# An attention and mixture-of-experts layer: the small transfers of the score maxima issued by ScalarE instead of SyncE

## What is computed

```
h   = layernorm(x)
q,k,v = h @ Wq, h @ Wk, h @ Wv        # 16 heads of size 64
p   = softmax(causal(q @ k.T / 8))    # 512 x 512 per head
y   = layernorm(h + concat(p @ v) @ Wo) * gamma + beta
x   = x + y
h2  = layernorm(x)
w   = top 8 of 32 experts of softmax(h2 @ gate.T), renormalised
x   = x + sum over experts of w_e * (up_e(h2) * silu(gate_e(h2))) @ down_e.T
```

## Time and profile before

| | kernel before |
|---|---|
| median of 3 runs | 1696.54 us |
| the profiled execution, device time | 1698.83 us |
| its span | 1697.0 us |
| PE busy | 1611.1 us (95%) |
| DVE busy | 1428.4 us (84%) |
| POOL busy | 1413.8 us (83%) |
| ACT busy | 1399.0 us (82%) |
| granted TensorE clock | 0.99 of full speed |
| DMA queues in use | one, 53.6% of the 16 engines' span |

### The profile page before, as it was taken

The page is one execution under the profiler, slowest core; times in us unless marked ns, Lnnn a source line. Parts: engine busy times, 40 slices in busy tenths (PEclk is TensorE's granted clock), DMA queues, the critical chain, the costliest instruction groups (busy, mean ns, idle before and its releaser), DMA issues.

```text
span 1697.0 us, 56373 instructions
## 1 busy us (share of the span) xinstructions
PE 1611.1 (95%) x21209; PEld 1104.6 (65%) x21209; DVE 1428.4 (84%) x4461; ACT 1399.0 (82%) x2371; POOL 1413.8 (83%) x1183
## 2 busy tenths in 40 slices
PE   4899999999999999999999999999999999999968
PEld 1476666667666666676667666666666666666645
DVE  7889789798888988888898888989888898888745
ACT  3999888888988888798888988888888888988852
POOL 0687897979889797997979889797998979889884
PEclk8899999999999999999999999999999999999989
DMA  9754544746556384544646555374654646355423
GB/s 252 162 115 109 145 115 127 170 116 157 123 135 140 103 183 102 155 111 129 161 115 163 124 133 136 107 185 115 155 111 131 146 120 163 86 145 139 112 85 108
DMA packets 213902, 228.55 MB, mean 135 GB/s; under 512 B 20480, under 2 KB 178432, under 8 KB 213376
## 3 DMA queue, kind: packets, MB, share of 16 engines
q1 hardware_dynamic: 213632, 224.94, 53.6%
HBM read 84.89 MB, written 5.24 MB: 53 GB/s over the span
## 4 chain that ended last, share of the span: by engine, by line
PE 35%; POOL 30%; issue 10%; SPq 8%; DMA 8%; ACT 7%; DVE 3%; POOLq 0%; ACTq 0%; DVEq 0%
POOL p_lo L1484 10%; PE bank_r L393 8%; POOL expert_room L1499 8%; POOL halves L1508 8%; PE bank_s L393 8%; PE bank_x L393 5%; PE bank_u L393 4%; PE bank_v L393 4%; PE bank_g L393 4%; DMA expert_room<-comb_rows 3%; DMA score_ops<-rowmaxT 3%; SPq L317 2%; SPq L316 2%; SPq L315 2%; ACT p L850 2%
## 5 line engine op out<-in xcount | busy, mean ns | idle before, releaser
L1484 POOL TENSOR_TENSOR p_lo<-p,p_hi 128x1280 f16<-128x1280 f32 x256 | 671.3, 2623 | 111.8 <-ACT p_hi L783 110.9
L850 ACT ACTIVATE p<-bank_s,back 128x512 f32<-128x512 f32 (+1 forms) x768 | 457.7, 613 | 88.1 <-PE bank_s L393 51.4
L393 PE MATMUL bank_s<-score_ops 128*128 128x62 f16 (+10 forms) x4096 | 398.7, 233 | 19.8 <-DMA score_ops<-rowmaxT 15.7
L393 PEld LDWEIGHTS bank_s<-score_ops 128*128 128x128 f16 x4096 | 275.2, 97 | 176.6 <-ACT p L850 34.1
L783 ACT ACTIVATE p_hi<-p 128x1280 f16<-128x1280 f32 x256 | 324.2, 1266 | 3.4 <-PE bank_r L393 1.2
L1499 POOL TENSOR_TENSOR expert_room<-expert_room 128x512 f32<-128x512 f32 x240 | 304.8, 1275 | 18.0 <-DMA expert_room<-comb_rows 12.4
L1508 POOL TENSOR_TENSOR halves<-expert_room,halves 128x512 f16<-128x512 f32 x240 | 277.4, 1160 | 2.4 <-ACT halves L783 1.6
L1125 DVE CUSTOM_DVE_ANT_0 max_junk<-bank_r,mask 128x512 f16<-128x512 f32 (+3 forms) x401 | 183.3, 490 | 20.6 <-PE bank_g L393 17.9
L393 PE MATMUL bank_x<-w_hi,halves 128*128 128x128 f16 x1920 | 195.8, 219 | 3.4 <-POOL halves L1508 3.3
L783 ACT ACTIVATE halves<-expert_room 128x512 f16<-128x512 f32 x240 | 150.3, 627 | 29.7 <-POOL expert_room L1499 15.2
L393 PE MATMUL bank_x<-w_lo,halves 128*128 128x128 f16 x960 | 171.7, 219 | 0.0
(11 more groups left out here) (287 smaller groups left out, 5018.0 us busy)
## 6 DMA issues: line engine op xcount, KB each, us to landing
score_ops<-nat SPq DMA_DIRECT2D x256, 256.0 KB, 3.9
score_ops<-nat SPq DMA_DIRECT2D x512, 128.0 KB, 3.9
expert_room<-comb_rows SPq DMA_DIRECT2D x240, 256.0 KB, 3.5
xt<-in_x SPq DMA_DIRECT2D x16, 256.0 KB, 4.7
xb<-in_x SPq DMA_DIRECT2D x16, 256.0 KB, 4.0
out_y<-expert_room SPq DMA_DIRECT2D x16, 256.0 KB, 3.6
score_ops<-comb_rows SPq DMA_DIRECT2D x16, 256.0 KB, 5.1
expert_room<-in_gate_up SPq DMA_DIRECT2D x1, 2048.0 KB, 10.6
```

The lines of the kernel that those rows point to most:

```text
L393: return pe.matmul(dst, lhsT, rhs, start=start, stop=stop, skip_group_check=shared)
L850: act.activation(p32[:, h % P_SLOTS, at:at + cols], bank[score_bank(h, u)][:, 0:cols], ACT.Exp, scale=back[:, SC_SCORE:SC_SCORE + 1]).then ...
L1484: pool.tensor_tensor(p_lo[:, slot, :], p32[:, slot, :], p_hi[:, slot, :], ALU.subtract).then_inc(p_lo_done, 1)
```

## The change

`place_max` leaves SP's program and enters ACT's, with the same waits and the same two transfers. Every call of `copy_maxima(m, g, b)` in ACT's list (64 of them) is now directly followed by `place_max(m, g)`, and the 64 calls are taken out of SP's list. Nothing else is moved.

```diff
         @block.sync
-            def place_max(m, g):
-                wait(sp, score_mm, UNITS * 2 * (m * PAIRS + 2 * g + 1 - SLOTS + 1))
-                if m == 0:
-                    for slot in range(2 * g, min(2 * g + 2, SLOTS)):
-                        sp.wait_ge(rows_filled[slot], 32)
-                sp.wait_ge(rowmaxT_ready, m * QUADS + g + 1)
-                for k in range(2):
-                    home = QB[E:E + MAX_ROWS, slot_of(m, 2 * g + k)].rearrange("a b (c p) -> a (b c) p", c=C)
-                    sp.dma_start(home, rowmaxT[16 * k:16 * k + 16, :]).then_inc(max_placed[g], 16)
...
             for n in range(2, B - 2):
-                load_x(n + 2); place_max(n, 1); spread_weights(n - 2, 15); place_qk(n, 5); place_max(n, 2)
+                load_x(n + 2); spread_weights(n - 2, 15); place_qk(n, 5)
...
-                place_max(n, 3); spread_weights(n - 1, 5); spread_weights(n - 1, 6); spread_weights(n - 1, 7)
+                spread_weights(n - 1, 5); spread_weights(n - 1, 6); spread_weights(n - 1, 7)
...
-                place_max(n + 1, 0); spread_weights(n - 1, 9); spread_weights(n - 1, 10); spread_weights(n - 1, 11)
+                spread_weights(n - 1, 9); spread_weights(n - 1, 10); spread_weights(n - 1, 11)
...
         @block.scalar
+            def place_max(m, g):
+                wait(act, score_mm, UNITS * 2 * (m * PAIRS + 2 * g + 1 - SLOTS + 1))
+                if m == 0:
+                    for slot in range(2 * g, min(2 * g + 2, SLOTS)):
+                        act.wait_ge(rows_filled[slot], 32)
+                act.wait_ge(rowmaxT_ready, m * QUADS + g + 1)
+                for k in range(2):
+                    home = QB[E:E + MAX_ROWS, slot_of(m, 2 * g + k)].rearrange("a b (c p) -> a (b c) p", c=C)
+                    act.dma_start(home, rowmaxT[16 * k:16 * k + 16, :]).then_inc(max_placed[g], 16)
...
-                exps(n, 2, 1); exps(n, 2, 2); copy_maxima(n, 1, U); p_high(n, 2); gate_tanh(n - 2, 13, R1)
+                exps(n, 2, 1); exps(n, 2, 2); copy_maxima(n, 1, U); place_max(n, 1); p_high(n, 2); gate_tanh(n - 2, 13, R1)
...
-                exps(n, 7, 1); copy_maxima(n, 2, R1); exps(n, 7, 2); residual_apply(n - 1); p_high(n, 7)
+                exps(n, 7, 1); copy_maxima(n, 2, R1); place_max(n, 2); exps(n, 7, 2); residual_apply(n - 1); p_high(n, 7)
...
-                unit_high(n - 1, 1); gate_tanh(n - 1, 4, G); copy_maxima(n, 3, R1); o_high(n, 4, V); exps(n, 11, 1)
+                unit_high(n - 1, 1); gate_tanh(n - 1, 4, G); copy_maxima(n, 3, R1); place_max(n, 3); o_high(n, 4, V); exps(n, 11, 1)
...
-                copy_maxima(n + 1, 0, V); exps(n, 15, 2); gate_tanh(n - 1, 9, U); qk_high(n + 1, 6, R0)
+                copy_maxima(n + 1, 0, V); place_max(n + 1, 0); exps(n, 15, 2); gate_tanh(n - 1, 9, U); qk_high(n + 1, 6, R0)
```

More of the change, by code:

```diff
@@ L372, in _ @@
             keep_weights(13); spread_weights(13, 0); spread_weights(13, 1); place_qk(14, 7); spread_weights(13, 2)
-            spread_weights(13, 3); spread_weights(13, 4); place_max(14, 3); spread_weights(13, 5); place_qk(15, 0)
-            load_xb(14); spread_weights(13, 6); place_max(15, 0); place_qk(15, 1); spread_weights(13, 7)
+            spread_weights(13, 3); spread_weights(13, 4); spread_weights(13, 5); place_qk(15, 0)
+            load_xb(14); spread_weights(13, 6); place_qk(15, 1); spread_weights(13, 7)
@@ L375, in _ @@
             spread_weights(13, 8); place_qk(15, 2); spread_weights(13, 9); place_qk(15, 3); spread_weights(13, 10)
-            spread_weights(13, 11); spread_weights(13, 12); place_max(15, 1); spread_weights(13, 13); place_qk(15, 4)
-            spread_weights(13, 14); spread_weights(13, 15); place_qk(15, 5); store(13); place_max(15, 2)
+            spread_weights(13, 11); spread_weights(13, 12); spread_weights(13, 13); place_qk(15, 4)
+            spread_weights(13, 14); spread_weights(13, 15); place_qk(15, 5); store(13)
@@ L378, in _ @@
             place_qk(15, 6); keep_weights(14); spread_weights(14, 0); spread_weights(14, 1); spread_weights(14, 2)
[L379 removed]
+            spread_weights(14, 3); spread_weights(14, 4); spread_weights(14, 5); place_qk(15, 7)
             spread_weights(14, 6); spread_weights(14, 7); spread_weights(14, 8); spread_weights(14, 9); load_xb(15)
@@ L902, in _ @@
             v_high(0, 0, U); v_high(0, 1, V); halve_rest(3); qk_high(0, 4, R0); v_high(0, 2, U); v_high(0, 3, R1)
-            qk_high(0, 5, R0); qk_high(0, 6, U); v_high(0, 4, V); copy_maxima(0, 0, R1); v_high(0, 5, G); halve_rest(4)
+            qk_high(0, 5, R0); qk_high(0, 6, U); v_high(0, 4, V); copy_maxima(0, 0, R1); place_max(0, 0); v_high(0, 5, G); halve_rest(4)
             halve_rest(5); exps(0, 0, 0); exps(0, 0, 1); qk_high(0, 7, R1); exps(0, 0, 2); exps(0, 1, 0); halve_rest(6)
@@ L906, in _ @@
             halve_rest(7); qk_high(0, 10, V); p_high(0, 1); exps(0, 2, 0); v_high(0, 7, U); exps(0, 2, 1); exps(0, 2, 2)
-            copy_maxima(0, 1, G); p_high(0, 2); qk_high(0, 11, R0); exps(0, 3, 0); exps(0, 3, 1); qk_high(0, 12, V)
+            copy_maxima(0, 1, G); place_max(0, 1); p_high(0, 2); qk_high(0, 11, R0); exps(0, 3, 0); exps(0, 3, 1); qk_high(0, 12, V)
             input_apply(1); exps(0, 3, 2); exps(0, 4, 0); halve_rest(8); p_high(0, 3); exps(0, 4, 1); exps(0, 4, 2)
             qk_high(0, 13, U); p_high(0, 4); qk_high(0, 14, R1); exps(0, 5, 0); exps(0, 5, 1); h_high(1, V)
-            qk_high(0, 15, U); o_high(0, 0, G); exps(0, 5, 2); halve_rest(9); exps(0, 6, 0); copy_maxima(0, 2, U)
+            qk_high(0, 15, U); o_high(0, 0, G); exps(0, 5, 2); halve_rest(9); exps(0, 6, 0); copy_maxima(0, 2, U); place_max(0, 2)
             p_high(0, 5); exps(0, 6, 1); halve_rest(10); qk_high(1, 0, U); exps(0, 6, 2); o_high(0, 1, V); p_high(0, 6)
@@ L913, in _ @@
             exps(0, 8, 2); o_high(0, 2, V); p_high(0, 8); qk_high(1, 2, G); exps(0, 9, 0); qk_high(1, 3, R0)
-            exps(0, 9, 1); exps(0, 9, 2); v_high(1, 0, U); exps(0, 10, 0); copy_maxima(0, 3, V); p_high(0, 9)
+            exps(0, 9, 1); exps(0, 9, 2); v_high(1, 0, U); exps(0, 10, 0); copy_maxima(0, 3, V); place_max(0, 3); p_high(0, 9)
             exps(0, 10, 1); v_high(1, 1, R1); o_high(0, 3, U); exps(0, 10, 2); v_high(1, 2, V); p_high(0, 10)
@@ L918, in _ @@
             exps(0, 13, 0); exps(0, 13, 1); exps(0, 13, 2); o_high(0, 4, U); p_high(0, 13); exps(0, 14, 0)
-            o_high(0, 5, G); exps(0, 14, 1); exps(0, 14, 2); copy_maxima(1, 0, R1); qk_high(1, 6, R0); p_high(0, 14)
+            o_high(0, 5, G); exps(0, 14, 1); exps(0, 14, 2); copy_maxima(1, 0, R1); place_max(1, 0); qk_high(1, 6, R0); p_high(0, 14)
             exps(0, 15, 0); exps(0, 15, 1); qk_high(1, 7, R1); exps(0, 15, 2); p_high(0, 15); exps(1, 0, 0)
@@ L922, in _ @@
             exps(1, 1, 0); exps(1, 1, 1); exps(1, 1, 2); o_high(0, 7, V); v_high(1, 4, R0); p_high(1, 1); exps(1, 2, 0)
-            exps(1, 2, 1); qk_high(1, 10, R1); exps(1, 2, 2); copy_maxima(1, 1, R0); p_high(1, 2); exps(1, 3, 0)
+            exps(1, 2, 1); qk_high(1, 10, R1); exps(1, 2, 2); copy_maxima(1, 1, R0); place_max(1, 1); p_high(1, 2); exps(1, 3, 0)
             v_high(1, 5, R0); exps(1, 3, 1); qk_high(1, 11, U); exps(1, 3, 2); residual_apply(0); p_high(1, 3)
@@ L927, in _ @@
             o_high(1, 1, V); exps(1, 5, 2); exps(1, 6, 0); qk_high(1, 14, G); p_high(1, 5); gate_tanh(0, 0, V)
-            exps(1, 6, 1); qk_high(1, 15, U); exps(1, 6, 2); copy_maxima(1, 2, V); gate_tanh(0, 1, G); exps(1, 7, 0)
+            exps(1, 6, 1); qk_high(1, 15, U); exps(1, 6, 2); copy_maxima(1, 2, V); place_max(1, 2); gate_tanh(0, 1, G); exps(1, 7, 0)
             p_high(1, 6); route(0); exps(1, 7, 1); exps(1, 7, 2); h_high(2, R0); p_high(1, 7); exps(1, 8, 0)
@@ L932, in _ @@
             unit_high(0, 0); exps(1, 10, 0); gate_tanh(0, 4, V); p_high(1, 9); unit_high(0, 1); o_high(1, 3, R1)
-            v_high(2, 0, G); exps(1, 10, 1); gate_tanh(0, 5, U); copy_maxima(1, 3, V); qk_high(2, 2, R0); exps(1, 10, 2)
+            v_high(2, 0, G); exps(1, 10, 1); gate_tanh(0, 5, U); copy_maxima(1, 3, V); place_max(1, 3); qk_high(2, 2, R0); exps(1, 10, 2)
             unit_high(0, 2); exps(1, 11, 0); p_high(1, 10); v_high(2, 1, R0); exps(1, 11, 1); exps(1, 11, 2)
@@ L938, in _ @@
             qk_high(2, 4, R0); o_high(1, 5, V); exps(1, 14, 2); unit_high(0, 4); gate_tanh(0, 8, G); exps(1, 15, 0)
-            qk_high(2, 5, U); unit_high(0, 5); copy_maxima(2, 0, R0); p_high(1, 14); gate_tanh(0, 9, U); unit_high(0, 6)
+            qk_high(2, 5, U); unit_high(0, 5); copy_maxima(2, 0, R0); place_max(2, 0); p_high(1, 14); gate_tanh(0, 9, U); unit_high(0, 6)
             o_high(1, 6, G); exps(1, 15, 1); gate_tanh(0, 10, V); exps(1, 15, 2); p_high(1, 15); unit_high(0, 7)
@@ L973, in _ @@
                 p_high(n + 1, 1); gate_tanh(n - 1, 12, G); exps(n + 1, 2, 0); input_apply(n + 2)
-            exps(14, 2, 1); copy_maxima(14, 1, U); gate_tanh(12, 13, G); unit_high(12, 11); exps(14, 2, 2)
```

(13 more changed lines are left out.)

14 lines of the change are left out of this document (7 added, 7 removed).

## The result

The changed kernel takes 1760.1 us, the median of four runs (1756.2 to 1762.2). The kernel before, run beside it, takes 1696.9 us. The ratio is 1.037, with a 95% interval of 1.035 to 1.039. The change costs 63 us. The forecast was 1728 us, with a range that ended at 1760 us.

What follows compares the result with a forecast made beforehand. PE was busiest (978 of 1000 us), with several hand-written orders tight at once. Delays of 83 us less 15.7 gave 67; about half, 32, on 1698.83 gave 1731, then 1728 us for the runs' median; range 1688 to 1760 us.

Steps and rivals of the forecast that it cites:

- The table of covers: At sequence 8, ACT's 1.56 us stall less each quad's slack: 5.2 us per sequence, 83 us for 16.
- The price of an issue on ACT: Behind each maxima copy, ACT's wait plus two issues: 0.17 + 1.39 = 1.56 us per quad, 100 us in 64.
- The lower bound: Behind each copy on ACT: about 0.17 us per quad, for the wait alone.
- the cheap case: ACT's queue takes the transfer over and ACT goes on: 11 us of stall, half counted, 1684 us; chance 0.10.
- the factor of one half: Of 67 us of delays at POOL, PE and ACT after the gain, only half reaches the end: 34 us.
- The dearer rival's second price: ACT's issues meet SP's, adding 37 us of stall, and all delays reach the end: 1764 us and up; rival's chance 0.20.
- The gain: At PE, sooner issues remove the waits for the maxima's landing: 15.7 us, the upper value, taken in full.
- SP's freedom: On SP's queue, transfers behind `place_max` could go sooner: up to 12.4 us of POOL's waits, taken as nothing.

Runs made afterwards that it cites:

- The four single runs: Kernel before with one quad of each sequence issued by ACT, the rest by SP: quads 0 to 3 took 1696.05, 1709.62, 1719.39, 1713.39 us.
- The copies kernel: Kernel before, SP issuing as before; ACT waits for each copy of the maxima, then makes three unneeded 32 x 512 copies: 1795.1 us, ratio 1.0612.
- twice the issues: Changed kernel with ACT issuing two more transfers of the same rows into DRAM, four issues per quad: 1856.9 us, ratio 1.0978 on the kernel before.

## Why the prediction was wrong

**The table of covers: right at quads 2 and 3, misread at quad 1, open at quad 0.** The table said 1.56, 1.24, 1.34 and 1.08 us per sequence for quads 2, 3, 1 and 0. The profile after shows 1.58 us at POOL for quad 2 and 1.22 us at POOL for quad 3, and the runs with these quads alone confirm them in time.

At quad 1 the cover was larger than 0.22 us. These are the rows of the kernel before at the same place:

```profile
838.56 0.95 PEld L393 LDWEIGHTS bank_s<-score_ops 128*128 128x128 f16 x12
...
840.75 0.10 PEld L393 LDWEIGHTS bank_s<-score_ops 128*128 128x128 f16 x1 [0.54 <-ACT p L850]
```

The twelve weight loads of before are the eight and the four of the trace after, and only the four wait there for the `exps` that, before, had ended at 838.55. If the eight took 0.72 us before as well, the four began at about 839.28, an estimate from these rows: the cover was about 0.7 us. After the change they wait 0.96 us. Of the second wait, 0.66 us, 0.54 us stood there before. So quad 1 costs PE about 0.96 + 0.12 = 1.08 us per sequence, 17 us in 16 and not 21.

**The price of an issue on ACT: right.** 1.56 us per quad was taken, and 1.57 us is in the rows of quad 2. The lower bound (the issue is handed over and costs ACT nothing) had no part in it. Two slips in the bounds did no harm: the longest issue on SP was 4.3 us, at the start, and not 2.42 us; and the cheap case, which counts half the stall, would decide at 0.49 us of stall per quad and so at 0.32 us for both issues, not at 0.25 us. By the Trainium skill, Perfetto Trace Analysis, section "DMA Instruction — HWDGE (DVE, Sync)", the sequencer is free only when the descriptors are made, and the trace agrees: ACT's next row starts 0.05 us behind the end of its second issue (893.45 against 893.40). The shared descriptor generator of that section would make an issue longer while SP issues, too; 11 of ACT's 128 issues took over 900 ns, up to 1320 ns, each while SP was issuing, and on SP none of them had taken over 786 ns. But all 128 together took 88 us on ACT against 87 us on SP, and quad 0 alone cost next to nothing. The Trainium skill, DMA: Bandwidth & Descriptors, section "Issuing engines are not separate DMA queues", calls this time usually small. Here the 128 issues are 88 us of ACT's time, and the kernel lost 63 us.

**The step that failed is the factor of one half.** The prediction had 83 us of delays less 15.7 us of gain, 67 us, and then wrote "I choose half, for want of a row that tells". (It then took 32 us, where half of 67 is 34.) Quads 2 and 3 show the failure most plainly: alone they cost 25.4 and 19.4 us, where the delays in full are 25 and 20 us and half of them 12 and 10 us. The four single runs add up to 62.5 us and the whole to 63.2 us: 67 us without the factor is within 4 us of both. That close a fit of the sum is in part luck, since its term for quad 1 is too large (21 us, against 17 by the rows), its term for the gain (15.7 us, see below) is not shown, and quad 0 came out 7 us cheaper than its own sum. The argument for the half was that delays at POOL and at PE lie partly side by side and that the chain is on one of them at a time. But the covers had already been taken off. The copies come 23 to 32 us apart, one behind another, so the delays do not lie side by side. That a delay is not made up later fits PE's 2% of idle time, but no run tried it with more. The dearer rival's second price, 1764 us "if on top all delays reach the end", has nearly the right amount, under a mechanism (issues that meet) that is seen at 11 issues and adds about 1 us in all.

**The gain: its size is not shown.** PE's 15.7 us of waits were to go to nearly nothing, and 7.0 us are left. The old ones, 7.7 us at quad 0 and 8.0 us at quad 1, are down to 0.8 us, but that is no proof of a gain. With ACT only waiting and SP issuing as before, 8.8 us of them went too and the kernel was no faster; with the copies, all went. (Each of these counts is from one profiled execution; how much it differs between executions of one kernel was not measured.) The sooner issue was tried by itself only in SP's list: there it took away the 7.7 us at quad 0, and the kernel was 5 us faster. So no run supports counting all 15.7 us as gain.

Of the 7.0 us left, 6.2 us are new ones, at quad 2, where the kernel before had none:

```profile
890.95 0.61 SPq L315 DMA_DIRECT2D score_ops<-nat  x1
...
891.61 0.65 SPq L316 DMA_DIRECT2D score_ops<-nat  x1
...
892.30 0.99 SPq L317 DMA_DIRECT2D score_ops<-nat  x1
...
896.37 0.38 PE L383 MATMUL bank_s<-score_ops 128*128 128x512 f16 x1 [0.73 <-DMA score_ops<-rowmaxT]
```

Before, SP stood at quad 2's `place_max`, and its K and Q transfers came behind it. Now nothing holds them, and they go out around the small transfer. The copies kernel, with more standing still and SP's old order, has no such wait. The kernel with quad 2 alone on ACT has 5.9 us of them, and those with another quad alone have none at quad 2. That it is the K and Q transfers that delay the landing is read from the order of these rows; it was not tried by itself. I had priced SP's freedom at nothing or a gain, and its price has the other sign at this quad.

## What to carry to other kernels

Before a transfer is moved to an engine that computes, count its issues times the duration of one in the trace, and add it to that engine as standing still at that place. Then read, place by place, how long before its next partner the engine's result is ready; count what remains after this cover in full, and don't halve it without a row that shows why. Here, with every engine's order fixed and PE at 98% in the steady part, it reached the end in full at quads 2 and 3. Find the cover at the very instruction that needs the result: a row that merges twelve of them hid 0.5 us at quad 1. The idle time of the engine as a whole (298 us here) said nothing. Nor is another engine's wait that the change would take away a gain of that size: 8.8 us of such waits went in a run that won no time. If only a few transfers are late, move those in the queue that they are in, and look at what is pushed behind a waiting instruction.

## What the runs showed of the hardware that I had not expected

TensorE's granted clock is lower in the kernels with more stall. Its mean is 0.990 in the kernel before, 0.986 in the changed one, 0.980 in the one with copies and 0.968 in the one with twice the issues. In the last one 15 stretches of 20 us show a clock of 0.91, against 1, 3 and 8 in the other three. Two stretches of 5 us from it (the last three figures are the granted clock, the DMA share and GB/s):

```profile
335.00:340.00 5.00, 3.21 (x20) 1.36 (x18) 2.01 (x7) 1.97 (x6) 3.87 (x3) 1.00 0.96 218
340.00:345.00 5.00, 4.74 (x29) 2.83 (x30) 3.37 (x9) 3.40 (x5) 4.12 (x3) 0.66 0.35 121
```

TensorE worked 3.21 of 5 us in the first, and in the second the clock was granted at 0.66 on the mean, so part of it was at 1.2 GHz. If the stalls cause this, which is read from the order of the kernels and was not tried, it is a second cost of a stall. Its size can be bounded by an estimate: one less the mean clock, times the span, is 17 us in the kernel before, 25 us in the changed one, 36 us with copies and 60 us with twice the issues. So it is at most 8 of the 63 us of the change, 19 of the 103 us of the copies and 35 of the 102 us of the second pair of issues.

Three copies of 32 x 512 behind one another took 1.91 us, without the overlap of about 0.1 us that ACT's other rows show. I don't know why.
